# Self attention's queries and keys and the shared expert's gate and up produced turned, and three pieces of TensorE's order moved

## The reference

```python
Q = heads(Wq, bq); K = heads(Wk, bk)                     # self attention, heads of 16
scores = einsum('bhid,bhjd->bhij', Q, K) / sqrt(16)
QJ = einsum('bhid,hde->bhie', tanh(Q), J_attn)
scores = scores + lambda_attn * einsum('bhie,bhje->bhij', QJ, tanh(K))   # then a causal softmax
...
shared_out = silu(x @ shared_gate_w) * (x @ shared_up_w) @ shared_down_w
```

## Time and profile before

| | |
|---|---|
| median of 3 runs | 1328.34 us (1325.62 to 1330.13) |
| the profiled execution's own time | 1323.34 us |
| its span, first to last instruction | 1320.9 us |
| TensorE busy | 1159.4 us (88%), 20184 matmuls |
| VectorE busy | 980.3 us (74%) |
| ScalarE busy | 661.9 us (50%) |
| GpSimd busy | 450.4 us (34%) |
| mean granted TensorE clock | 0.957 |

### The profile page before, as it was taken

One profiled execution on the slowest core, in us unless ns is written; L12 is line 12 of the kernel. 1 busy time (PEld: TensorE's weight loads), 2 busy tenths in 40 slices (PEclk: granted clock), 3 DMA queues, 4 the chain that ended last, 5 costly groups with the idle time before them and its releaser, 6 DMA issues.

```text
span 1320.9 us, 49683 instructions
## 1 busy us (share of the span) xinstructions
PE 1159.4 (88%) x20184; PEld 927.4 (70%) x20184; DVE 980.3 (74%) x2496; ACT 661.9 (50%) x1441; POOL 450.4 (34%) x436
## 2 busy tenths in 40 slices
PE   4689999999999999999999999999999875899940
PEld 3577777777777777777777777777777654588830
DVE  6578888888888888888888788878887743465547
ACT  1455555555555555555555555555555532355520
POOL 1333333333333333333333333333333321255530
PEclk8899999999999999999999999999999986799975
DMA  4101111111111111121111111111110004586558
GB/s 162 41 23 46 51 51 50 51 51 51 50 51 50 51 51 35 35 97 37 35 35 35 34 35 35 34 35 35 35 39 15 14 14 135 150 246 169 156 190 269
DMA packets 82559, 91.80 MB, mean 69 GB/s; under 512 B 17248, under 2 KB 72544, under 8 KB 82016
## 3 DMA queue, kind: packets, MB, share of 16 engines
q1 hardware_dynamic: 70816, 65.41, 17.0%
q0 software_dynamic: 6912, 19.01, 4.0%
q10 hardware_dynamic: 4608, 4.20, 0.9%
HBM read 61.19 MB, written 33.78 MB: 72 GB/s over the span
## 4 chain that ended last, share of the span: by engine, by line
PE 67%; DVE 11%; issue 8%; ACT 8%; DMA 3%; POOL 1%; SPq 1%; DVEq 0%; ACTq 0%; POOLq 0%
PE ringB L492 17%; PE ringC L503 11%; PE oA L587 10%; DVE mx L1224 6%; PE banksS L788 5%; PE banksS L570 4%; ACT qT L876 4%; PE ringB L668 3%; PE oA L492 2%; DVE rz L1238 2%; ACT pT L920 2%; PE ringB L622 2%; DMA out<-ksq 2%; PE banksS L639 2%; PE banksS L563 2%
## 5 line engine op out<-in xcount | busy, mean ns | idle before, releaser
L1045 POOL TENSOR_TENSOR kn<-kc,rr 128x512 f32<-128x512 f32 x64 | 66.8, 1065 | 309.8 <-DVE rr L1212 309.8
L503 PE MATMUL ringC<-wx_kv,ct 128*128 128x256 f32 x512 | 158.6, 310 | 8.6 <-DVE ws_down L1366 6.1
L868 ACT ACTIVATE pt<-banksS 128x1024 f32<-128x1024 f32 x128 | 127.6, 1023 | 70.6 <-PE banksS L570 67.0
L1224 DVE TENSOR_REDUCE mx<-banksS 128x8 f32<-128x2048 f32 x64 | 146.4, 2287 | 0.9 <-PE banksS L544 0.9
L503 PE MATMUL ringC<-wx_kv_rest,ct 128*128 128x256 f32 x512 | 145.4, 284 | 0.0
L503 PE MATMUL ringC<-wx_kv,ct_rest 128*128 128x256 f32 x512 | 145.2, 284 | 0.1
L1039 POOL TENSOR_TENSOR sc<-sc,rz 128x1024 f32<-128x1024 f32 x32 | 62.4, 1949 | 197.4 <-DVE rz L1285 197.4
L503 PEld LDWEIGHTS ringC<-wx_kv,ct 128*128 128x128 f32 x512 | 97.9, 191 | 22.4 <-DVE ws_down L1366 6.2
L1082 POOL DMA_INDIRECT expert_rows<-kc,row_to x80 | 76.5, 956 | 69.1 <-DVE kc L1473 62.3
L503 PEld LDWEIGHTS ringC<-wx_kv_rest,ct 128*128 128x128 f32 x512 | 98.3, 192 | 0.1
L503 PEld LDWEIGHTS ringC<-wx_kv,ct_rest 128*128 128x128 f32 x512 | 98.1, 192 | 0.0
(11 more groups left out here) (226 smaller groups left out, 2938.7 us busy)
## 6 DMA issues: line engine op xcount, KB each, us to landing
ct_in<-in_ctxT SPq DMA_DIRECT2D x64, 256.0 KB, 3.0
pt<-rows_by_expert SPq DMA_DIRECT2D x80, 130.0 KB
rows_by_expert<-in_pad_rows SPq DMA_DIRECT2D x16, 260.0 KB
xt<-in_x SPq DMA_DIRECT2D x32, 128.0 KB, 3.3
rows_without_experts<-base SPq DMA_DIRECT2D x32, 128.0 KB
pt<-expert_rows SPq DMA_DIRECT2D x16, 256.0 KB, 3.8
out<-ksq ACTq DMA_DIRECT2D x32, 128.0 KB, 3.8
rows_by_expert<-in_dump_rows SPq DMA_DIRECT2D x1, 2080.0 KB
```

The source lines that it names most:

```text
L503: mm = pe.matmul(ringC[:, half * DIM:(half + 1) * DIM], left[:, p, k, j // 2, (j % 2) * P:(j % 2 + 1) * P], right[:, k, part * DIM:(part + ...
L868: act.activation(pt[:, g, :, :, :, :].rearrange("p i q c n -> p i (q c n)"), banksS[:, :, g * 256:(g + 1) * 256], ACT.Exp)\
L1045: pool.tensor_tensor(kn[:, 2 * jj:2 * jj + 2, :].rearrange("p j (h d) -> p (j h) d", d=HD), kc[:, 2 * jj:2 * jj + 2, :].rearrange("p j (h ...
L1224: dve.tensor_reduce(mx[:, 2 * r:2 * r + 2, :, 0].rearrange("p q i -> p i q"), banksS[:, :, :].rearrange("p i (q m) -> p i q m", q=2), AX.X ...
```

## The change

TensorE now computes the queries and keys transposed (weights `wa_qk` stationary, the rows moving: 8 products of 128 columns for 2 of 512), and the shared expert's gate and up in the same way. The transposes TQ, TK and ST go, with the copies `heads_in` and `gated_rows_in`. `self_mix` works on tanh of the queries alone (2 products for 4). The scores are now two accumulated parts (linear, and tanh with the mix), each with queries of even and odd heads side by side as 32x128 weights; ScalarE's new `queries_apart` and `mixed_in`, two instructions each, spread them with scales that hold zeros for the other head. In TensorE's list XT moves ahead of QK, X1 behind CNT, and QT ahead of PT0. `B_USES` has 13 entries for 16, and `claim` now looks back for the last use with the same bank number. Buffers, small constants and `laid_out` are refitted, one VectorE instruction of the setup goes (L1365), and two of the buffers that rows rest in during the experts are others. SyncE's and GpSimd's lists are as before; the loads of `rows` and `jmix` are smaller. The core of the diff:

```diff
 
 C_USES = (("K1", 2), ("XT", 2), ("Q", 2), ("V0", 2), ("CNT", 5), ("V1", 2), ("K0", 1))
-B_USES = (("NT", 4), ("O0", 5), ("O1", 5), ("WO", 5), ("QK", 4), ("TQ", 4), ("TK", 4), ("HT", 5), ("MIX", 4), ("RT", 5), ("GU", 5), ("ST", 5), ("VP", 4), ("Y", 5), ("PT0", 4), ("PT1", 4))
+B_USES = (("NT", 4), ("O0", 5), ("O1", 5), ("WO", 5), ("QK", 4), ("HT", 5), ("MIX", 4), ("RT", 5), ("GU", 5), ("VP", 4), ("Y", 5), ("PT0", 4), ("PT1", 4))
...
-    back = place_of[u] - banks
-    while back >= -2 * len(uses):
+    for back in range(place_of[u] - 1, -2 * len(uses) - 1, -1):
+        if back % len(uses) % banks != place_of[u] % banks:
+            continue
...
-        back -= banks
...
-        product(bankB("QK"), "QK", lambda k: x1T[:, k, :], wa_qk, 2 * DIM)
-
-    def heads_turned(b, p, u, side):
-        claim(pe, B_USES, B_BANKS, u, b)
-        pe.wait_ge(ev["tanh_ready"].sem, ev["tanh_ready"].of(b))
-        for q4 in range(QG):
-            mm = pe.transpose(bankB(u)[:, q4 * P:(q4 + 1) * P], qkn[:, side, 4 * q4:4 * q4 + 4, :].rearrange("p h d -> p (h d)"), ident[:, :])
-        mm.then_inc(full[u].sem, 1)
+        for f in range(2 * G):
+            for k in range(KD):
+                mm = pe.matmul(bankB("QK")[:, f * P:(f + 1) * P], wa_qk[:, k, f * P:(f + 1) * P], x1T[:, k, :],
+                               start=(k == 0), stop=(k == 1))
+        mm.then_inc(full["QK"].sem, 1)
...
-        pe.wait_ge(free["TQ"].sem, free["TQ"].of(b))
-        for q4 in range(QG):
-            mm = pe.matmul(bankB("MIX")[:, q4 * P:(q4 + 1) * P], jmix[:, q4, :], qk4[:, 0, q4, :], start=True, stop=True)
+        pe.wait_ge(ev["tanh_ready"].sem, ev["tanh_ready"].of(b))
+        for g in range(G):
+            mm = pe.matmul(bankB("MIX")[:, g * P:(g + 1) * P], jmix[:, g, :], qk_tanh[:, g, :], start=True, stop=True)
         mm.then_inc(full["MIX"].sem, 1)
...
+        pe.wait_ge(ev["linear_ready"].sem, ev["linear_ready"].of(b))
         pe.wait_ge(free["MIX"].sem, free["MIX"].of(b))
-        pe.wait_ge(free["TK"].sem, free["TK"].of(b))
...
-        for g in range(G):
-            for bb in range(2):
-                at = (2 * g + bb) * N
-                for odd in range(2):
+        for part, keys in enumerate((qk_linear, qk_tanh)):
+            for g in range(G):
+                for bb in range(2):
+                    at = (2 * g + bb) * N
                     for i in range(4):
-                        lo, q4 = 32 * i, 2 * g + odd
-                        mm = pe.matmul(banksS[odd * N:(odd + 1) * N, i, at:at + N], qm[lo:lo + 32, q4, bb * N:(bb + 1) * N],
-                                       qk4[lo:lo + 32, 1, q4, bb * N:(bb + 1) * N], start=False, stop=True, skip_group_check=True)
+                        lo = 32 * i
+                        mm = pe.matmul(banksS[:, i, at:at + N], q_parts[lo:lo + 32, part, 2 * g + bb, :],
+                                       keys[lo:lo + 32, G + g, bb * N:(bb + 1) * N], start=False, stop=(part == 1), skip_group_check=True)
         mm.then_inc(full["SS"].sem, 1)
...
-        product(bankB("GU"), "GU", lambda k: hT[:, k, :], ws_gu, 2 * DIM)
-
-    def gated_turned(d, p):
-        claim(pe, B_USES, B_BANKS, "ST", d)
-        pe.wait_ge(su_ready.sem, su_ready.of(d))
-        turned(bankB("ST"), "ST", su)
+        for f in range(2 * KD):
+            for k in range(KD):
+                mm = pe.matmul(bankB("GU")[:, f * P:(f + 1) * P], ws_gu[:, k, f * P:(f + 1) * P], hT[:, k, :],
+                               start=(k == 0), stop=(k == 1))
+        mm.then_inc(full["GU"].sem, 1)
...
-        pe.wait_ge(free["ST"].sem, free["ST"].of(d))
+        pe.wait_ge(su_ready.sem, su_ready.of(d))
...
         on(s, odd, 5, self_output)
+        on(s, odd, 2, rows_turned)
         on(s, odd, 4, self_qk)
-        on(s, odd, 2, rows_turned)
         on(s, odd, 3, rough_scores, 1)
         on(s, odd, 2, query_product)
-        on(s, odd, 4, heads_turned, "TQ", 0)
-        on(s, odd, 4, heads_turned, "TK", 1)
         on(s, odd, 3, maxima_turned)
         on(s, odd, 5, ffn_rows_turned)
...
-        on(s, odd, 5, gated_turned)
         on(s, odd, 4, self_scores)
...
         on(s, odd, 2, keys_turned)
-        on(s, odd, 3, cross_output)
         if s != TILES - 1 + 5:
             on(s, odd, 5, counts)
+        on(s, odd, 3, cross_output)
         on(s, odd, 5, down)
         on(s, odd, 2, context_product, "V1", 1, 1)
+        on(s, odd, 2, queries_turned)
         on(s, odd, 4, probs_turned, 0)
-        on(s, odd, 2, queries_turned)
         on(s, odd, 4, probs_turned, 1)
...
-    def gated_rows_in(d, p):
-        freed(act, full["Y"], d)
-        rows_of(suT, bankB("ST"), "ST", d)
...
-        act.activation(qkn[:, :, :, HD:2 * HD].rearrange("p s h d -> p (s h) d"), qkn[:, :, :, 0:HD].rearrange("p s h d -> p (s h) d"),
+        freed(act, full["MIX"], b)
+        freed(act, full["SS"], b)
+        act.activation(qk_tanh[:, :, :].rearrange("p a n -> p (a n)"), qk_linear[:, :, :].rearrange("p a n -> p (a n)"),
                        ACT.Tanh).then_inc(ev["tanh_ready"].sem, 1)
...
-    def heads_in(b, p, u, side):
-        act.wait_ge(full[u].sem, full[u].of(b))
-        freed(act, full[("MIX", "SS")[side]], b)
-        act.copy(qk4[:, side, :, :].rearrange("p q n -> p (q n)"), bankB(u)).then_inc(free[u].sem, 1)
+    def queries_apart(b, p):
+        act.wait_ge(free["QK"].sem, free["QK"].of(b))
+        freed(act, full["SS"], b)
+        for odd in range(2):
+            ins = act.activation(q_parts[:, 0, :, odd * N:(odd + 1) * N], qk_linear[:, 0:G, :].rearrange("p g (b n) -> p (g b) n", n=N),
+                                 ACT.Identity, bias=cols[:, 17:18], scale=cols[:, 15 + odd:16 + odd])
+        ins.then_inc(ev["linear_ready"].sem, 1)
 
     def mixed_in(b, p):
         act.wait_ge(full["MIX"].sem, full["MIX"].of(b))
         freed(act, full["SS"], b)
-        act.copy(qm[:, :, :].rearrange("p q n -> p (q n)"), bankB("MIX")).then_inc(free["MIX"].sem, 1)
+        for odd in range(2):
+            ins = act.activation(q_parts[:, 1, :, odd * N:(odd + 1) * N], bankB("MIX")[:, 0:DIM].rearrange("p (q n) -> p q n", n=N),
+                                 ACT.Identity, bias=cols[:, 17:18], scale=cols[:, (6, 18)[odd]:(7, 19)[odd]])
+        ins.then_inc(free["MIX"].sem, 1)
...
-        on(s, odd, 4, heads_in, "TQ", 0)
-        on(s, odd, 4, heads_in, "TK", 1)
+        on(s, odd, 4, queries_apart)
...
-        on(s, odd, 5, gated_rows_in)
...
-        freed(dve, full["TQ"], b)
-        freed(dve, full["TK"], b)
-        dve.tensor_tensor(qkn[:, :, :, 0:HD].rearrange("p s h d -> p (s h) d"), bankB("QK").rearrange("p (a d) -> p a d", d=HD),
-                          rows[:, 4:6, :].rearrange("p s (h d) -> p (s h) d", d=HD), ALU.add).then_inc(free["QK"].sem, 1)
+        freed(dve, ev["linear_ready"], b)
+        freed(dve, ev["tanh_ready"], b)
+        freed(dve, full["SS"], b)
+        dve.tensor_tensor(qk_linear[:, :, :], bankB("QK").rearrange("p (a n) -> p a n", n=P),
+                          cols[:, 11:15].unsqueeze(2).to_broadcast([P, 2 * G, P]), ALU.add).then_inc(free["QK"].sem, 1)
...
-            freed(dve, full["ST"], d)
-            dve.tensor_tensor(su[:, :], sg[:, :], bankB("GU")[:, DIM:2 * DIM], ALU.mult).then_inc(su_ready.sem, 1)
+            freed(dve, full["Y"], d)
+            dve.tensor_tensor(suT[:, :, :].rearrange("p k n -> p (k n)"), sg[:, :], bankB("GU")[:, DIM:2 * DIM], ALU.mult).then_inc(su_ready.sem, 1)
...
-            dve.tensor_scalar(jmix[:, :, :], jmix[:, :, :], cols[:, 6:7], None, ALU.mult)
```

More of the change, by code:

```diff
@@ L110, in perceiver_block @@
         wa_o = sb("wa_o", [P, KD, DIM])
-        jmix = sb("jmix", [P, QG, P])
+        jmix = sb("jmix", [P, G, P])
         w_route = sb("w_route", [P, KD, E])
@@ L114, in perceiver_block @@
         ws_down = sb("ws_down", [P, KD, DIM])
-        cols = sb("cols", [P, 11])
-        rows = sb("rows", [P, 6, DIM])
+        cols = sb("cols", [P, 19])
+        rows = sb("rows", [P, 4, DIM])
         ident = sb("ident", [P, P])
@@ L165, in perceiver_block @@
         x1T = sb("x1T", [P, KD, P])
-        qkn = sb("qkn", [P, 2, H, PAD])
-        qk4 = sb("qk4", [P, 2, QG, P])
-        qm = sb("qm", [P, QG, P])
+        qk_linear = sb("qk_linear", [P, 2 * G, P])
+        qk_tanh = sb("qk_tanh", [P, 2 * G, P])
+        q_parts = sb("q_parts", [P, 2, QG, 2 * N])
         v2 = sb("v2", [P, HP, 2, 2 * HD])
@@ L184, in perceiver_block @@
         sg = sb("sg", [P, DIM])
-        su = sb("su", [P, DIM])
         suT = sb("suT", [P, KD, P])
@@ L226, in perceiver_block @@
                    qn[:, :], v2[:, :, :, :].rearrange("p h o d -> p (h o d)"),
-                   qm[:, :, :].rearrange("p q n -> p (q n)"), wa_o[:, :, :].rearrange("p k d -> p (k d)"),
-                   jmix[:, :, :].rearrange("p q n -> p (q n)"), xt[:, :])
+                   qk_tanh[:, :, :].rearrange("p a n -> p (a n)"), wa_o[:, :, :].rearrange("p k d -> p (k d)"),
+                   wa_qk[:, 0, :], xt[:, :])
```

(17 more changed lines are left out.)

14 lines of the change are left out of this document (7 added, 7 removed).

## The result

The changed kernel takes 1395.0 us (median of 4 runs, 1378.3 to 1397.5) and the kernel before 1328.5 (4 runs): ratio 1.048, 95% interval 1.039 to 1.056. It is slower, as forecast, but by 66.5 us and not by 47.6, and lies outside the range. Its four runs scatter by 1.4%, those of before by 0.3%, and they go with the mean granted clock: 0.927 to 0.934 in the three long ones, 0.943 in the short one.

The account below looks back on a forecast made before the run. TensorE's work was taken as most of the time, with waits each step, MT's on VectorE's split-and-maximum chain. Terms sum to +1.71 us a step, x 29 = 49.6, less 2.0: +47.6, so 1376 us; range 1342 to 1390.

Parts of the forecast that it names:

- banks, NT and O1: Start of the step: NT's bank claim now waits for PT1's copy, so K1 and all behind come 0.57 us later.
- XT's place and QK turned: XT ahead of QK stalls 0.17 us and costs 0.26; QK as 16 narrow matmuls costs 0.08; together 0.50 us later.
- MIX halved: Self attention's mix with two products fewer: 0.18 us a step gained of its 0.45, since C0 waits for `shifted`.
- GU turned: Shared expert's gate and up computed transposed: 0.08 us a step later, priced as for QK.
- ST gone: Two transposes between V0 and SS go: 0.26 us a step earlier, on the path, their copy hidden.
- SS: Self attention scores with 32x128 weights for 32x64: 1.0 us a step later, weight loads setting the pace; the largest unknown.
- X1 behind CNT: CNT fills X1's wait of 0.51 us, but V1 then waits 0.5 for `rows_placed`: no change to the step, 0.
- QT ahead of PT0: `queries_in` starts behind `values` 1 on ScalarE, with QT's result there either way: 0.
- rival 3: Dearer: SS's loads and columns in sequence (+0.8 us a step more), or a lower clock at MT's wait; 1399 us, chance 0.08.
- The tail: Last steps, stages alone: transposes and copies that go are latency there; 2 us in all gained (0 to 4).
- SS costs nothing: Rival: moving columns set the pace of the self attention scores, adding nothing; +18 us, 1346 us, chance 0.17.
- Faster because TensorE's own work decides: Rival: VectorE's maximum is not what MT waits for, or the chain gives way elsewhere; 1309 us, chance 0.06.

## Why the prediction was right or wrong

**What bounds, and the centre of it: right.** The chain QK's last result, split, maximum, MT is 3.08 us after (531.66 to 534.74) for 3.07; MT's wait is 1.69, forecast "about 1.8". TQ and TK gave nothing by their going; what it cost, through the clock, is told below.

**The terms, forecast and measured** (us a step, against the same point of an undisturbed step):

| term | forecast | measured |
|---|---|---|
| banks, NT and O1 | +0.57 | +0.48 (timeline), 0.44 (undone) |
| XT's place and QK turned | +0.50 | +0.43; XT's place alone 0.33 |
| MIX halved | -0.18 | -0.18 |
| GU turned | +0.08 | +0.07 |
| ST gone | -0.26 | -0.26 |
| SS | +1.0 | +1.10 |
| X1 behind CNT | 0 | -0.19, 0.21 undone |
| QT ahead of PT0 | 0 | -0.10 undone |
| sum | +1.71 | +1.30 (the terms' own sum 1.35) |

Of the forecast's 0.41 too much, 0.3 are the two moves that I called nothing. *X1 behind CNT: 0* failed because I took `pos_u`'s end as fixed by `heads_out` 1 and `self_sums`; it also waited for CNT, by 0.18. *QT ahead of PT0: 0* failed because I read "behind `values` 1" from two rows 0.65 apart; they are 0.54 apart where QT is early, so QT was the one that came last. The bound of SS with loads and columns one after the other was added wrongly: 64 records of 0.038 less 0.84 are +1.6, not +1.8, which makes rival 3 about 1393. The forecast does not use it. The sign "steps of about 34.5 us" is the forecast on the mean step of before, 32.85; the mean step after is 35.14, the undisturbed one 33.81.

**The multiplication.** I compared 29 undisturbed steps with 29, but the real ones are longer: by 9.8 us in all before, and by 5.6 after where the clock has no part in it. Why less after, no run shows. So the mechanism's part of the result is 37.7 - 4.2 = +33.5 us, not +49.6.

**The clock: the step that made it wrong.** The sum has no term for TensorE's clock: it prices MT's new wait by its length alone, and holds all TensorE work at the pace of the rows before. Under rival 3 I wrote "a lower granted clock where MT waits 1.8 us", gave it, with the dearer SS, 0.08, and priced it together at 1399, near the result, because "no row of a full step prices the latter". The range ended below it. It was the largest single term, 33.0 us in the 29 steps; without it the time would have been about 1362, inside the range. The rows to price one fall by were there all the same: the kernel before has a granted clock of 0.69 between 1078 and 1100 us, where stages are alone and waits long, and MIX takes 2.08 us there for 1.06. They do not tell how many falls there would be. I had worked out that a step would hold 1.7 us of new waiting, and did not ask what else it costs. The shortfall of the step and the excess of the clock partly cancel, so that it was in part luck that 1376 lies only 19 us from the result.

**The tail: not as forecast.** Forecast -2; from the last MT on it is +1.7, with a granted clock of 0.82 before and 0.81 after over that stretch. It is one execution of each, and the same stretch is 6.3 us shorter in the one execution with the banks undone. So neither the forecast nor its reverse is shown.

**Rivals.** SS costs nothing: refuted by the row and by the halved columns. Faster because TensorE's own work decides: refuted, the row of VectorE stands; it comes true only when the maximum is moved ahead of the split, the banks are undone and two pieces of ScalarE's list are moved as well, which together is worth 1% against the kernel before.

## What to carry to other kernels

Before work is taken from the busiest engine, look at what waits at its end: where another engine's chain covers it to 0.3 us, the work is only filler, and what is won is won when the other engine's order is changed too. Price a new wait on TensorE twice, by its length and by the clock that may fall behind it, and where the trace then shows such falls and the wait can't be avoided, try cheap idle matmuls in it. A move that is "worth nothing" needs the releaser's own inputs read, one link further back.

## What the runs showed of the hardware that I had not expected

The granted clock fell though TensorE was busy 92% of the step (31.06 of 33.85 us). A fall of about 7 us costs 3 us or a little more here, and the four times of the changed kernel scatter 1.4% with their mean clock, those of the kernel before 0.3%. Eight idle transposes a step made a kernel 35 us faster, two repeated products 22 us. A wait of 1.68 us lowered the clock in one kernel, and one of 1.73 did not in the other; what in the surroundings decides is shown only as far as the work just behind the wait goes. 32x64 weights in eight tiles take 0.013 us a record and 32x128 weights in four 0.030, and the latter is the same with 32 and with 64 moving columns.
